# First cross-attention of a two-block kernel: reciprocal behind the next maximum, transposes ahead of the values, one stage less between them

## What is computed

```python
x = x + xattn0(layernorm(x), ctx, ctx, Wq, bq, Wk, bk, Wo, bo, key_padding_mask)   # 8 heads of 4, 154 keys
x = x + ffn0(layernorm(x), ...)        # causal conv, self-attention of 16 heads, mixture of 4 experts
x = x + xattn1(layernorm(x), ctx, row_mask, Wq, Wkv, Wout, bout)                   # 16 heads of 64
x = x + ffn1(layernorm(x), ...)

# xattn0, for each sequence:
scores = einsum('bhqd,bhkd->bhqk', Q @ Wq.T + bq, K @ Wk.T + bk) / 2   # masked keys: -inf
out = einsum('bhqk,bkd->bqhd', softmax(scores), V).reshape(b, tq, 8 * 128) @ Wo.T + bo
```

## Time and profile before

| what | us |
|---|---|
| median of 3 runs | 351.3 |
| lowest, highest | 349.03, 351.62 |
| span of the profiled execution | 346.5 |

### The profile page before, as it was taken

How to read it: one execution, slowest core, us unless ns; L and a number is a source line. 1 busy time by engine, 2 the same in 40 slices (tenths; PEclk the granted TensorE clock), 3 DMA queues, 4 the chain that set the end, 5 groups by cost and what they waited for, 6 DMA issues and landing times.

```text
span 346.5 us, 6818 instructions
## 1 busy us (share of the span) xinstructions
PE 321.4 (93%) x2406; PEld 228.1 (66%) x2406; DVE 240.7 (69%) x607; ACT 215.8 (62%) x633; POOL 121.6 (35%) x151
## 2 busy tenths in 40 slices
PE   7888999998999998988999999998999999999885
PEld 2336887664566544435654898995688687877774
DVE  4987766594899977852651464368788877887575
ACT  1478886165237364565668744855766676686994
POOL 3525563101630033330522161410586535535300
PEclk9999999999999999999999999999999999999999
DMA  7690000057777300009002002300100000000002
GB/s 207 204 264 2 2 0 2 6 161 218 214 240 195 81 2 0 2 9 340 25 8 78 0 17 70 84 2 1 55 15 18 0 2 0 3 1 0 2 0 63
DMA packets 21591, 22.46 MB, mean 65 GB/s; under 512 B 3606, under 2 KB 18358, under 8 KB 21558
## 3 DMA queue, kind: packets, MB, share of 16 engines
q1 hardware_dynamic: 19750, 19.93, 19.8%
q0 software_dynamic: 512, 1.05, 1.0%
q10 hardware_dynamic: 1296, 1.05, 0.9%
HBM read 14.22 MB, written 7.60 MB: 63 GB/s over the span
## 4 chain that ended last, share of the span: by engine, by line
PE 58%; DVE 25%; ACT 10%; issue 4%; DMA 1%; POOL 1%; ACTq 0%; DVEq 0%; POOLq 0%
PE PS L1312 49%; DVE mB L835 9%; PE PS L1366 6%; ACT big L1122 3%; ACT big L1288 3%; DVE big L669 2%; DMA X<-in_x 1%; DVE XN L625 1%; DVE big L642 1%; DVE mraw L634 1%; ACT big L1096 1%; DVE U L625 1%; DVE stats L614 1%; DVE mraw L658 1%; ACT big L1240 1%
## 5 line engine op out<-in xcount | busy, mean ns | idle before, releaser
L1312 PE MATMUL PS<-big 128*128 128x128 f32 (+10 forms) x592 | 94.7, 308 | 6.7 <-DVE big L642 1.7
L1312 PEld LDWEIGHTS PS<-big 128*128 128x128 f32 (+3 forms) x592 | 58.0, 150 | 38.3 <-issue 11.3
L511 POOL TENSOR_TENSOR big<-big,urec 128x1024 f32<-128x1024 f32 x24 | 45.6, 1898 | 62.8 <-DVE urec L676 45.6
L1122 ACT ACTIVATE big<-big 128x154 f32<-128x154 f32 x192 | 60.4, 319 | 6.7 <-DVE big L669 5.0
L1240 ACT ACTIVATE big<-PS 128x1024 f32<-128x1024 f32 (+3 forms) x64 | 42.2, 704 | 25.5 <-PE PS L1312 25.1
L835 DVE TENSOR_REDUCE mB<-PS 128x2 f32<-128x256 f32 (+5 forms) x90 | 50.1, 624 | 7.2 <-PE PS L1312 7.2
L1096 ACT ACTIVATE big<-PS 128x1280 f32<-128x1280 f32 (+2 forms) x30 | 32.6, 1091 | 32.5 <-PE PS L1366 30.0
L1312 PE MATMUL PS<-cstb 128*128 128x128 bf16 x192 | 37.8, 220 | 0.0
L1312 PE MATMUL PS<-kkC,XT 128*128 128x462 f32 (+1 forms) x96 | 36.0, 510 | 1.7 <-DVE big L669 1.7
L499 POOL TENSOR_TENSOR rstd<-ve,minus_half 128x4 f32<-128x4 f32 (+2 forms) x13 | 13.2, 1016 | 69.0 <-DVE ve L620 69.0
L1122 ACT ACTIVATION_READ_ACCUMULATOR big<-big 128x1 f32 x192 | 36.3, 189 | 0.0
(11 more groups left out here) (192 smaller groups left out, 489.4 us busy)
## 6 DMA issues: line engine op xcount, KB each, us to landing
scr_qk<-big SPq DMA_DIRECT2D x12, 384.0 KB, 3.5
big<-scr_qk SPq DMA_DIRECT2D x16, 288.0 KB
big<-in_wv SPq DMA_DIRECT2D x1, 2048.0 KB, 8.1
scr_x<-zrow SPq DMA_DIRECT2D x2, 448.0 KB, 6.5
scr_y<-big SPq DMA_DIRECT2D x2, 448.0 KB, 3.6
X<-in_x ACTq DMA_DIRECT2D x2, 256.0 KB, 3.8
big<-in_A_WoT ACTq DMA_DIRECT2D x1, 512.0 KB, 4.7
cw<-in_C_Wk SPq DMA_DIRECT2D x1, 512.0 KB, 5.3
```

What stands on the lines that cost most here:

```text
L511: pool.tensor_tensor(pn[:, 0:GH * P].rearrange("p (h k) -> p h k", h=GH), Pt[u % 3][:, :, 0:KM], r.to_broadcast([P, GH, KM]), ALU.mult).th ...
L1122: i = act.activation(Pt[u % 3][:, h, :], Pt[u % 3][:, h, :], ACT.Exp, accum_out=usum[:, u % 3, h:h + 1])
L1312: return pe.matmul(o, lhsT, rhs, start=start, stop=stop)
```

## The change

On DVE the reciprocal of unit u-1 moves from behind the shifts of unit u to behind the maximum of unit u. `constants` is cut in four parts behind units 0, 2, 3 and 4, and the second sequence's queries, which ACT scaled before, are scaled by DVE behind unit 1. On PE the order within u becomes scores of u, transposes of u-2, values of u-3. The 5 and the 4 `hold_clock` matmuls go, one V·Wo job moves from behind unit 1 to behind unit 0, and `queries_A(1)` goes behind the last of them. Jobs 6 to 8 of `fold_C` move behind `queries_keys(0)`, `turn("b", XN, (0,))` goes ahead of jobs 3 to 5, and `queries_keys(0)` no longer waits for the last `add_tile`. ACT follows suit.

```diff
@@ DVE units_A
+                def row_sums(v):
+                    dve.wait_ge(unit_exp["A"], v + 1)
+                    dve.reciprocal(urec[:, v % 3, :], usum[:, v % 3, :]).then_inc(unit_rec["A"], 1)
...
                         own(dve.tensor_reduce(mraw[:, u % 2, :].rearrange("p (g j) -> p g j", j=2), s, AX.X, ALU.max))
+                        if u >= 1:
+                            row_sums(u - 1)
                         own.wait()
...
-                    if u >= 1:
-                        v = u - 1
-                        dve.wait_ge(unit_exp["A"], v + 1)
-                        dve.reciprocal(urec[:, v % 3, :], usum[:, v % 3, :]).then_inc(unit_rec["A"], 1)
-                    if u >= 4:
-                        add_tile("A", u - 4)
+                    else:
+                        row_sums(u - 1)
+                    if u >= 3:
+                        add_tile("A", u - 3)
@@ DVE constants
+            def second_queries():
+                dve.wait_ge(s4_ready, 1)
+                dve.wait_ge(q4_mm, 2)
+                dve.tensor_scalar(Q4[:, 1, :], PS[:, Q4_BANK[1], :], s4, b4, ALU.mult, ALU.add).then_inc(q4_ready, 1)
...
-            units_A({0: constants, NT - 1: lambda: ln_u_stats(0), NT: lambda: ln_b_stats(0)})
-            add_tile("A", NT - 3)
+            units_A({0: first_bias, 1: second_queries, 2: lambda: x_plus(1, rowv[:, R_BO, :]), 3: bf16_constants, 4: row_biases,
+                     NT - 1: lambda: ln_u_stats(0), NT: lambda: ln_b_stats(0)})
@@ ACT
+            units("A", {0: lambda: copy_A(2, len(PREA)), NT: lambda: copy_C(0, F_UNIT[0]), NT + 1: second_gap})
@@ PE units_A
-                for u in range(NT + 4):
+                for u in range(NT + 3):
...
+                    if 2 <= u <= NT + 1:
+                        turn_weights("A", u - 2)
                     if u == 2:
                         pe.wait_ge(q4_ready, B)
                         hold_clock(OUT_BANK["A"], 8)
-                    elif u == 3:
-                        hold_clock(OUT_BANK["A"], 5)
-                    if u >= 4:
-                        weigh_values("A", u - 4, vwAm, vwAr)
-                    if 2 <= u <= NT + 1:
-                        turn_weights("A", u - 2)
+                    if u >= 3:
+                        weigh_values("A", u - 3, vwAm, vwAr)
...
                 turn("a", XN, (1,))
-                hold_clock(6, 4)
+                fold_A(2, 3)
...
             def second_gap():
+                turn("b", XN, (0,))
                 fold_C(F_UNIT[0], F_UNIT[1])
-                turn("b", XN, (0,))
...
-                else:
-                    pe.wait_ge(tile_added["A"], NT)
...
-            fold_C(F_UNIT[2], F_LN)
+            fold_C(F_UNIT[1], F_LN)
```

31 lines of the change are left out of this document (13 added, 18 removed).

## The result

| | before | after |
|---|---|---|
| median of 4 runs each, us | 350.39 | 345.79 |
| lowest, highest | 349.03, 351.62 | 344.94, 346.73 |
| span of the profiled execution | 346.5 | 344.6 |
| device time of that execution | not shown | 346.56 |

The ratio is 0.9882, with a 95% interval of 0.984 to 0.9924: the changed kernel is 1.2% faster. The prediction was 348.9 us in a range of 346.9 to 351.7, with 0.74 on "within 1%".

A forecast was written before the change was run, and what follows sets the result against it. Stage A was taken as bound by a 4.25 us circle of DVE's shifts, PE's scores and DVE's maximum. Queries 3.6 us sooner, cut by jobs 6 to 8 on PE, gave 2.4: 351.3 - 2.4 = 348.9 us, range 346.9 to 351.7.

The forecast's parts named there:

- The base: Whole kernel: the median stays 4.8 us above the profiled span, so 344.1 us of span becomes 348.9 us.
- The size of the stage's gain: Stage A to the second sequence's layernorm: its transposes on PE come at 78.7 instead of 81.14, 2.4 us gained.
- The new circle: Stage A, shifts to shifts through ACT's exponentials and DVE's reciprocal: 4.49 us a unit against 4.25, +0.24 us.
- The start won and given back: First units of stage A: 0.95 us won at unit 1 (shifts' end at 20.84), nothing left by unit 7.
- The group of values less: End of stage A: PE has one values group less ahead of the queries, which start at 62.4 instead of 66.00.
- PE as the late one: Queries to second layernorm's transposes: PE needs 16.3 us with jobs 6 to 8, DVE 15.1, so PE ends last.
- Rival 1: Stage A: transposes wait for POOL, circle of 4.8 us a unit, nothing won, median 351.0 us; chance 15%.
- Rival 2: Second layernorm: jobs 6 to 8 find cover, DVE sets the time, 3.6 to 4.1 us gained, median 347.4; chance 14%.
- Rival 3: Stage A: DVE's clamp waits for POOL's product, 2.06 us a unit, median 363.3 us; chance 6%.
- Rival 4: First units: with 9 filling matmuls gone the clock falls to 1.2 GHz, costing 3.8 us, median 352.7; chance 5%.
- The chance of faster by over 1%: Whole kernel: 0.18 that it is faster by over 1%, from rival 2 and a little of the forecast's upper edge.
- DMAs start by semaphores, so all of it moves along: Behind the second layernorm: order on every engine is unchanged, so the 2.4 us gain reaches the end whole.

The follow-up runs named there:

- recip_back: Changed kernel with only DVE's reciprocal back behind the shifts; 356.25 us against 350.88, ratio 1.0146.
- ln24: after_hold with the second layernorm's transposes two jobs sooner; 346.38 us against 346.68.
- start_part: Kernel before with only the start changed: constants in four pieces, second queries on DVE, V·Wo job and `queries_A(1)` moved; 352.2 us against 351.57, ratio 1.0019.
- before again: Kernel before, run again unchanged as a kernel of its own; 352.11 us against 351.57, ratio 0.9997.
- before_hold: Kernel before with 4 filling matmuls ahead of the second sequence's self-attention; 350.61 us against 351.31, ratio 0.999.
- tail_part: Kernel before with only the tail changed: first layernorm's transposes earlier, jobs 6 to 8 behind the queries, no wait for last `add_tile`; 353.51 us against 351.57, ratio 1.004.
- order_part: Kernel before with only the new order within units, 5 filling matmuls gone, constants and tail as before; 352.86 us against 351.57, ratio 1.0016.
- start_and_order: Changed kernel with its tail put back as before; 347.89 us against 350.88 for the kernel before, ratio 0.9915.
- after_hold: Changed kernel with 4 filling matmuls ahead of the second sequence's self-attention; 346.68 us against 351.31 for the kernel before, ratio 0.9874.
- after_again: Changed kernel, run again unchanged; 348.06 us against 351.31 for the kernel before, ratio 0.9906.
- no_filling: Changed kernel without the last 8 filling matmuls, at unit 2; 351.18 us against 350.88 for the kernel before, ratio 0.9986.
- folds_back: Changed kernel with jobs 6 to 8 back ahead of unit 7's values and the queries; 348.9 us against 350.88 for the kernel before, ratio 0.9943.

## Why the prediction was wrong

**The base: the step that failed.** "The median is 4.8 us above the span, and if this stays, it becomes 351.3 - 2.4 = 348.9 us." It did not stay: the changed kernel's median is 345.79 - 344.6 = 1.2 us above its profiled span. The 4.8 us were taken as time around the instructions, and that time measures 2.0 us (1.9 to 2.3 in every execution of every kernel for which both numbers are there). The other 2.8 us were the distance of one profiled execution from the median of others, which the sum carried over as if it belonged to the kernel. The runs show two parts of it: falls of the clock near 155 and 187 us, some 1.6 us each, which the profiled execution did not have, and at equal clock a profiled execution that was shorter than any rerun (346.5 us against 347.0 and more, with medians from 347.9 to 348.3).

Of the 3.1 us between 348.9 and 345.79, 0.9 are the base itself, whose fourth run brought 351.3 down to 350.39. The trace's gain accounts for 0.1: 0.5 more in the stage, 0.4 lost at 116 us. The remaining 2.1 us are a difference between the first medians that no trace shows. With 2.0 us around the forecast's own span, 344.1 + 2.0 = 346.1, the sum would have come out near the measured median, and that is partly luck: it takes the changed kernel's typical execution to be as short as the profiled one. It was in the first comparison; in the repeat the median was 348.06, which lies in the stated range.

**The size of the stage's gain (0.5 us).** 2.91 us instead of 2.4. Of this, 0.3 us come from the shifts of unit 7, at 47.68 instead of 48.0: the 0.2 us charged for the collision with POOL were nothing, since the delay of the transposes (0.45 us) ended in PE's slack, and the circle was 0.02 us shorter in six of seven (unit 4's took 4.53 us, behind the two bf16 constants). Another 0.1 us comes from layernorm "u", which took 1.47 us behind 52.42 where I gave it 1.6 behind 52.7, and the last 0.1 from the way between queries and second transposes, 16.22 us instead of 16.3. The rest kept its distance: transposes 57.71 (58.1), queries 62.01 (62.4), second transposes 78.23 (78.7).

**Right by its steps.** The new circle (4.49, measured 4.47) and the short wait for ACT (0.15, measured 0.18). The start won and given back: 20.84 forecast for unit 1, measured 20.81. The group of values less: 62.4 for the queries, measured 62.01. PE as the late one, with 16.3 us from the queries to the second transposes: measured 16.22.

**Rival 1** (circle of 4.8 us) did not come; it takes a late reciprocal, as recip_back shows. **Rival 2** gave a median (347.4) nearer to the truth than the forecast's, but for a reason that isn't there: DVE is ready 1.2 us before PE. ln24 shows what it takes. **Rival 3** did not come: DVE's issue at 0.12 us beats POOL's at 0.28 in all seven units. start_part shows its price, 1.75 us for one instruction of 128x8. **Rival 4** did not come with 9 matmuls less, and comes with 17 less, at 1.5 us instead of 3.8: the fall lasts 3.41 us, in which PE at half its clock can lose at most 1.7 us of work. I had made a whole unit slow.

**The chance of faster by over 1%.** As shares, 2.4 us of 351.3 are 0.7%, and 2.91 of 350.39 are 0.8%. The interval of the measured ratio (0.984 to 0.9924) holds the latter, on the near side of 1%, and so does that of the repeat, 0.9906 (0.9869 to 0.9944). On which side of 1% this change lies the measurements don't settle; such a case deserved more than 0.18.

**"DMAs start by semaphores, so all of it moves along": 0.4 us wrong.** The loss at 116 us is a transfer that did not move along. The loss goes with the packet of instructions and not with the reloads. From profiles, in us behind the first maximum, and the loss up to the last maximum of the block against before:

| | reloads start | packet of instructions ends | last small load moved | loss |
|---|---|---|---|---|
| before | 12.08 | 23.96 | 27.2 | 0 |
| before again, before_hold, start_part, tail_part | 12.26 to 12.53 | 23.92 to 24.11 | 27.2 | 0.0 |
| order_part | 12.72 | 26.33 | 27.6 | 0.09 |
| start_and_order | 12.95 | 26.34 | 27.6 | 0.09 |
| after, after_hold, after_again | 12.84 to 12.91 | 26.62, 26.63, 26.71 | 27.9 to 28.0 | 0.38, 0.38, 0.46 |
| no_filling | 13.32 | 26.88 | 28.2 | 0.64 |
| recip_back | 13.02 | 27.29 | 27.7 | 0.40 |
| ln24 | 12.94 | 27.32 | 27.7 | 0.43 |
| folds_back | 13.55 | 27.74 | 28.1 | 0.84 |

By the reloads alone start_and_order should lose more than the changed kernel, and it loses 0.3 us less. With the packet the rows fall into three groups. Where it ends at 24 us, ahead of the small loads, nothing is lost. Where it ends between 26.33 and 26.88, SP's third issue is drawn out (1.01 to 1.56 us instead of 0.60) and the last load is through 1.29 us behind the packet in each. Where it ends later, that issue has its usual length and the last load is through 0.38 us behind the packet in each. PE's matmul starts 0.9 to 1.2 us behind the last of it in each. This is read from traces alone; no run moved the packet or took a transfer away to prove it.

**Open.** What sets the time of the packet of instructions: it comes beside the small loads in every kernel with PE's new order of units, and 2.5 to 3.9 us sooner in the others. And of the 4.60 us between the first medians, 2.91 less 0.4 are accounted for by the trace; the remaining 2 us did not all repeat (3.25 us between the second medians), and they would have to lie behind 154 us, where executions of one kernel differ by as much.

## What to carry to other kernels

Before a gain is set against a median, ask of what clock level the profiled execution was, and how it compares with others of the same kernel. Time less span of one and the same execution is a small constant (2.0 us here); the distance between one profile and the median of others is not. Price an edit in the circle of the engines that ends last, and then ask again at the next hand-over which engine has become late: here PE became the late one, and the moves in the tail, the layernorm's transposes ahead of three jobs above all, cost 0.4 us of a 3.3 us gain. Parts of a reordering may hold each other up: order, start and tail alone were each no better than the kernel before, and the first two together carry all of the gain.
